# Three order sums of linear attention moved to accumulating transfers, with a reordered VectorE and ScalarE schedule

## The reference, cut to what matters

```python
h = _layernorm(x) * (1 + ca) + sa
q, k, v = split(h @ W_in.T)                      # 16 heads of 16 channels
xq, xk = clip(q / 4), clip(k / 4)
Tq, Tk = _cheb(xq), _cheb(xk)
Tv = Tk * v
kv_prefix = jnp.cumsum(Tv, axis=2)               # over the tokens, for each order
ks_prefix = jnp.cumsum(Tk.sum(axis=-1), axis=2)
num = (Tq * kv_prefix * beta).sum(axis=3)        # sum over the orders 1 to 5
den = (Tq.sum(axis=-1) * ks_prefix * beta).sum(axis=3)
x = x + ga * (num / (den + 1e-7)) @ W_out.T
h = _layernorm(x) * (1 + cb) + sb
activation = jnp.sqrt(jax.nn.softplus(h @ routing_W.T + expert_bias))
top_vals, top_idx = jax.lax.top_k(activation, 2)  # weights of the experts
x = x + gb * (shared(h) + sum over the experts of weight * expert(h))
```

## Time and profile before

| | |
|---|---|
| time, median of 3 runs | 1087.46 us (1085.91 to 1087.97) |
| profiled execution | 1086.55 us, span 1084.9 us |
| PE busy | 948.9 us (87%), 4889 matmuls |
| DVE busy | 947.9 us (87%), 1465 instructions |
| ACT busy | 472.5 us (44%) |
| POOL busy | 516.6 us (48%) |
| POOL L630, two of the sums | 32 of 2364 ns |
| DMA queues | 34.18 MB, about 13% of the time of 16 engines |

### The profile page before, as it was taken

How to read it: one execution, slowest core, us unless ns; L and a number is a source line. 1 busy time by engine, 2 the same in 40 slices (tenths; PEclk the granted TensorE clock), 3 DMA queues, 4 the chain that set the end, 5 groups by cost and what they waited for, 6 DMA issues and landing times.

```text
span 1084.9 us, 15500 instructions
## 1 busy us (share of the span) xinstructions
PE 948.9 (87%) x4889; PEld 678.4 (63%) x4889; DVE 947.9 (87%) x1465; ACT 472.5 (44%) x702; POOL 516.6 (48%) x615
## 2 busy tenths in 40 slices
PE   3864749998998989999999999898999999889996
PEld 3643436675756666675757576675757576656774
DVE  1498989999999999999999999999999999999432
ACT  4334335372635445362635444362635445441431
POOL 2032646646645546536645546536645445454210
PEclk9876869999999999999999999999999999999999
DMA  8100001020202002020202011020202010020211
GB/s 270 45 1 20 20 0 50 1 59 1 69 1 59 1 9 60 0 58 0 69 0 58 0 16 53 0 58 0 69 0 39 0 24 25 1 39 1 44 21 20
DMA packets 31517, 34.18 MB, mean 32 GB/s; under 512 B 1299, under 2 KB 30430, under 8 KB 31462
## 3 DMA queue, kind: packets, MB, share of 16 engines
q1 hardware_dynamic: 21410, 22.72, 6.3%
q0 software_dynamic: 8448, 8.39, 5.9%
q10 hardware_dynamic: 1604, 2.46, 0.7%
HBM read 16.77 MB, written 16.79 MB: 31 GB/s over the span
## 4 chain that ended last, share of the span: by engine, by line
PE 32%; DVE 30%; issue 18%; POOL 11%; ACT 3%; DVEq 1%; POOLq 0%; ACTq 0%
PE ring L1257 13%; PE acc L1394 7%; DVE feat L945 7%; PE tr L1342 4%; PE tr L1310 4%; DVE feat L966 3%; POOL feat L625 2%; DVE hid L1094 2%; DVE feat L962 2%; DVE feat L1004 2%; DVE feat L1001 2%; POOL ms L357 1%; PE tr L1248 1%; DVE route L1083 1%; PE cfb L1368 1%
## 5 line engine op out<-in xcount | busy, mean ns | idle before, releaser
L784 ACT ACTIVATE hid<-ring,b1row 128x512 f32<-128x512 f32 x144 | 98.6, 685 | 163.5 <-PE ring L1257 163.5
L630 POOL TENSOR_TENSOR feat<-feat 128x1024 f32<-128x1024 f32 x32 | 75.6, 2364 | 197.7 <-DVE feat L962 152.8
L1394 PE MATMUL acc<-w,hid 128*128 128x256 f32 x640 | 156.6, 392 | 0.0
L1394 PEld LDWEIGHTS acc<-w,hid 128*128 128x128 f32 x640 | 117.1, 191 | 28.0 <-issue 14.5
L945 DVE TENSOR_TENSOR_SCAN feat<-zero,carry,feat 128x512 f32<-128x512 f32 x80 | 113.1, 1453 | 0.0
L945 DVE TENSOR_TENSOR_SCAN feat<-zero,feat 128x512 f32<-128x512 f32 x80 | 109.9, 1413 | 0.0
L1094 DVE TENSOR_TENSOR hid<-hid,cfb 128x512 f32<-128x512 f32 x128 | 86.2, 673 | 25.7 <-PE cfb L1368 25.3
L1257 PE MATMUL ring<-n2H,w1H 128*128 128x512 f32 x288 | 101.9, 436 | 0.0
L1257 PE MATMUL ring<-n1H,winH 128*128 128x512 f32 x192 | 67.3, 433 | 38.7 <-ACT hid L784 24.9
L742 ACT ACTIVATE feat<-ring,bqkv 128x512 f32<-128x512 f32 x96 | 65.7, 686 | 71.5 <-PE ring L1257 71.5
L382 ACT ACTIVATE ntok<-xin,ms 128x256 f32 (+1 forms) x64 | 33.2, 589 | 138.5 <-POOL ms L361 138.5
(11 more groups left out here) (169 smaller groups left out, 2238.7 us busy)
## 6 DMA issues: line engine op xcount, KB each, us to landing
xin<-in_L_attn_x SPq DMA_DIRECT2D x16, 512.0 KB, 5.5
out<-x SPq DMA_DIRECT2D x16, 512.0 KB, 4.5
out<-fin POOLq DMA_DIRECT2D x16, 512.0 KB, 6.2
gates<-gate_rows SPq DMA_DIRECT2D x16, 128.0 KB, 4.8
feat<-in_L_wmod SPq DMA_DIRECT2D x1, 1536.0 KB, 14.1
feat<-in_L_attn_W_in SPq DMA_DIRECT2D x1, 768.0 KB, 9.5
const<-in_constants ACTq DMA_DIRECT2D x1, 690.5 KB, 4.3
fin<-in_constants ACTq DMA_DIRECT2D x1, 512.0 KB, 5.2
```

What stands on the lines that cost most here:

```text
L630: g.tensor_tensor(f(W + 2 * n), f(W + 2 * n), f(W + 2 * n + 1), ALU.add).then_inc(added, 1)
L784: a.activation(hid[:, e % NG], ring[bank][:, :], ACT.Silu, bias=b1row[:, e:e + 1]).then_inc(ring_copied, 1)
L1394: last = mm(acc[t // 2][:, t % 2], x[:, t * P:(t + 1) * P], w[:, e // 2], start=False, stop=(e == E), skip_group_check=True)
```

## The change

The adds of POOL go, and so does one of DVE's two. Three transfers on POOL's queue take their place: W += W+1 after two products, W+4 += W+3 after four, and, once both have landed, W += W+4. The third stands behind `exps` in POOL's list, ahead of `inv_std` of the first norm. DVE adds only W+2, after the fifth product. Orders are now scanned as 1, 2, 4, 5, 3. The copies of the last column of p = 0 are three (`carry_over`) instead of five. DVE's order changes: both scans of orders 4 and 5 stand behind `expert(3)`, their products behind `expert(4)`, then `low(4)`, `logit_parts`, the denominators, the weighing of order 3, the first norm's statistics and the clips; `finish_numerator` stands ahead of `expert(8)`. The softplus polynomial has five fitted coefficients in place of eight of the series: 10 instructions instead of 13. On ScalarE `normalise_first` moves from ahead of `silu(5)` to behind `high(6)`, and the squares of the keys from behind `silu(8)` to behind `silu(6)`.

```diff
+LOG1P = (2.0000000076817583, 0.666663216413768, 0.40024595230747134, 0.2796515774481493, 0.2815777836368378)
@@ GpSimd
             def add_orders(i, p, n):
-                pool.wait_ge(products, ND * number(i, p) + 2 * n + 2)
-                g.tensor_tensor(f(W + 2 * n), f(W + 2 * n), f(W + 2 * n + 1), ALU.add).then_inc(added, 1)
+                c = number(i, p)
+                if n < 2:
+                    pool.wait_ge(products, ND * c + 2 * n + 2)
+                else:
+                    pool.wait_ge(added[0], 16 * c + 16)
+                    pool.wait_ge(added[1], 16 * c + 16)
+                into, of = ((W, W + 1), (W + 4, W + 3), (W, W + 4))[n]
+                pool.sem_inc(sum_begun, 1)
+                g.dma_start(f(into), f(of), accum_op=ALU.add).then_inc(added[n], 16)
...
                     add_orders(i, p, 0)
+                    add_orders(i, p, 1)
+                if st["second"]:
+                    exps(*later(i, p, -1))
+                if st["attn"]:
+                    add_orders(i, p, 2)
                 if st["norm"]:
                     inv_std(pool, 0, *later(i, p, 2))
                 if st["second"]:
-                    exps(*later(i, p, -1))
                     scores(*later(i, p, -1))
-                if st["attn"]:
-                    add_orders(i, p, 1)
@@ ScalarE, in step
-                if st["norm"]:
-                    normalise_first(act, *later(i, p, 2))
                 silu(5)
                 high(4)
                 copy("v0")
                 copy("v1")
                 silu(6)
+                if qkv:
+                    for which in range(3):
+                        square(*nxt, 0, which)
                 silu(7)
                 high(6)
+                if st["norm"]:
+                    normalise_first(act, *later(i, p, 2))
                 silu(8)
                 if qkv:
-                    for q in range(2):
-                        for which in range(3):
-                            square(*nxt, q, which)
+                    for which in range(3):
+                        square(*nxt, 1, which)
@@ VectorE
-            ORDERS = (0, 1, 3, 2, 4)
+            ORDERS = (0, 1, 3, 4, 2)
+            BY_WEIGHT = (0, 1, 3, 2)
+            NCARRY, CARRIED = 3, {0: 1, 1: 1, 3: 2, 4: 2, 2: 3}
...
+            def carry_over(i, p, k):
                 if p == 0:
-                    dve.wait_ge(scanned, ND * c + j + 1)
-                    v.tensor_copy(carry[:, n], feat[:, W + n, :, CT - 1]).then_inc(carried, 1)
+                    at, n, j = ((0, 2, 1), (3, 2, 3), (2, 1, 4))[k]
+                    dve.wait_ge(scanned, ND * number(i, p) + j + 1)
+                    v.tensor_copy(carry[:, at:at + n], feat[:, W + at:W + at + n, :, CT - 1]).then_inc(carried, 1)
...
                 dve.wait_ge(products, ND * c + ND)
-                dve.wait_ge(added, 2 * c + 1)
-                v.tensor_tensor(f(W), f(W), f(W + 4), ALU.add).then_inc(numerator, 1)
-                dve.wait_ge(numerator, 2 * c + 1)
-                dve.wait_ge(added, 2 * c + 2)
+                dve.wait_ge(added[2], 16 * c + 16)
                 v.tensor_tensor(f(W), f(W), f(W + 2), ALU.add).then_inc(numerator, 1)
@@ VectorE, step, from expert(3) on (without the conditions)
                 expert(3)
+                prefix(i, p, 2)
+                prefix(i, p, 3)
+                expert(4)
+                carry_over(i, p, 1)
+                order_product(i, p, 2)
+                order_product(i, p, 3)
+                low(4)
+                logit_parts(*prev)
+                den_key_sums(i, p)
+                den_products(i, p)
+                weigh(i, p, 3)
                 token_stats(dve, 0, *after2)
-                weigh(i, p, 3)
-                prefix(i, p, 2)
                 clip(*nxt, use, 0)
                 clip(*nxt, use, 1)
-                logit_parts(*prev)
-                expert(4)
-                den_key_sums(i, p)
-                den_products(i, p)
-                low(4)
+                expert(5)
                 softplus(*prev)
-                prefix(i, p, 3)
-                expert(5)
-                order_product(i, p, 2)
-                order_product(i, p, 3)
                 invert(i, p)
                 expert(6)
+                prefix(i, p, 4)
+                low(6)
+                carry_over(i, p, 2)
+                order_product(i, p, 4)
+                expert(7)
                 combine_weights(*prev)
-                low(6)
-                prefix(i, p, 4)
-                expert(7)
-                order_product(i, p, 4)
+                finish_numerator(i, p)
                 expert(8)
-                finish_numerator(i, p)
                 divide(i, p)
```

More of the change, by code:

```diff
@@ L240, in build @@
         products = sem("order_products")
-        added = sem("orders_added")
+        added = [sem(f"orders_added{n}") for n in range(3)]
+        sum_begun = sem("order_sums_begun")
         numerator = sem("numerator")
@@ L260, in build @@
         ffn_gated = sem("ffn_gated")
-        NLOG, NSOFT, NCF, NSPLIT, NMV = 7, 13, 3, 7, 11
+        NLOG, NSOFT, NCF, NSPLIT, NMV = 7, 10, 3, 7, 11
         late_products, late_biases, late_weights = (sem(f"late_{n}") for n in ("bias_products", "biases", "weights"))
@@ L623, in weigh_order_5 @@
                 pool.wait_ge(odd_ready, 4 * c + 2)
-                ge(pool, numerator, 2 * c)
+                ge(pool, numerator, c)
                 g.tensor_tensor(f(W + 4), f(KT5), f(V0), ALU.mult).then_inc(weighted5, 1)
             def add_orders(i, p, n):
-                pool.wait_ge(products, ND * number(i, p) + 2 * n + 2)
-                g.tensor_tensor(f(W + 2 * n), f(W + 2 * n), f(W + 2 * n + 1), ALU.add).then_inc(added, 1)
+                c = number(i, p)
[7 more added lines that the diff above has]
+                g.dma_start(f(into), f(of), accum_op=ALU.add).then_inc(added[n], 16)
             def exps(i, p):
@@ L700, in step @@
                 if st["second"]:
-                    exps(*later(i, p, -1))
                     scores(*later(i, p, -1))
-                if st["attn"]:
-                    add_orders(i, p, 1)
-                if st["second"]:
                     split_weights(*later(i, p, -1))
@@ L752, in square @@
                     act.wait_ge(clipped, 2 * c + q + 1)
+                    ge(act, summed, 2 * c - 1 + q)
                     if q == 0:
-                        ge(act, summed, 2 * c)
+                        ge(act, weighted, (ND - 1) * c)
+                        ge(act, weighted5, c)
+                    else:
                         ge(act, products, ND * c)
@@ L938, in prefix @@
                 if n < 4:
-                    dve.wait_ge(weighted, (ND - 1) * c + j + 1)
+                    dve.wait_ge(weighted, (ND - 1) * c + BY_WEIGHT.index(n) + 1)
                 else:
@@ L942, in prefix @@
                 if p:
-                    dve.wait_ge(carried, ND * i + j + 1)
+                    dve.wait_ge(carried, NCARRY * i + CARRIED[n])
                 for h in range(KD):
@@ L1007, in divide @@
                 c = number(i, p)
-                dve.wait_ge(numerator, 2 * c + 2)
+                dve.wait_ge(numerator, c + 1)
                 for k in range(KD):
@@ L1062, in softplus @@
                 v.tensor_tensor(b(Z2), b(Z), b(Z), ALU.mult).then_inc(soft_steps, 1)
[L1063 to L1069, removed]
+                v.scalar_tensor_tensor(out=b(PL), in0=b(Z), scalar=LOG1P[4], in1=b(Z),
+                                       op0=ALU.mult, op1=ALU.mult).then_inc(soft_steps, 1)
+                for k, m in enumerate((3, 2, 1)):
+                    dve.wait_ge(soft_steps, at + 5 + k)
+                    v.scalar_tensor_tensor(out=b(PL), in0=b(PL), scalar=LOG1P[m], in1=b(Z2),
                                            op0=ALU.add, op1=ALU.mult).then_inc(soft_steps, 1)
-                dve.wait_ge(soft_steps, at + 11)
-                v.scalar_tensor_tensor(out=b(PL), in0=b(PL), scalar=2.0, in1=b(Z),
+                dve.wait_ge(soft_steps, at + 8)
+                v.scalar_tensor_tensor(out=b(PL), in0=b(PL), scalar=LOG1P[0], in1=b(Z),
                                        op0=ALU.add, op1=ALU.mult).then_inc(soft_steps, 1)
-                dve.wait_ge(soft_steps, at + 12)
+                dve.wait_ge(soft_steps, at + 9)
                 v.tensor_tensor(b(PL), b(PL), b(MX), ALU.add).then_inc(soft_steps, 1)
@@ L1140, in step @@
                 low(2)
+                if attn_:
+                    carry_over(i, p, 0)
                 if second:
@@ L1146, in step @@
                 expert(3)
+                if attn_:
+                    prefix(i, p, 2)
+                    prefix(i, p, 3)
+                expert(4)
+                if attn_:
+                    carry_over(i, p, 1)
+                    order_product(i, p, 2)
+                    order_product(i, p, 3)
+                low(4)
+                if second:
+                    logit_parts(*prev)
```

(15 more changed lines are left out.)

6 lines of the change are left out of this document (3 added, 3 removed).

## The result

The changed kernel takes 1103.49 us (median of 4 runs, 1101.39 to 1104.84) against 1086.68 us before on the same terms: ratio 1.0153, 95% interval 1.0131 to 1.0174. It is slower by 1.5%; the forecast was faster by 2.2%, and the time lies outside the range. Yet most of what the forecast counted did come. First its page: busy time and share of the span by engine; the new transfers' instruction on POOL (busy us, mean ns, idle before it); their KB each and median us to landing.

A forecast was written before the change was run, and what follows sets the result against it. PE and DVE were taken to bound each step together. From 1086.55 us, less 19.8 for the loop's steps and 9 for those outside, plus 5 for PE's clock, came 1062.8, called 1063, range 1055 to 1071.

The forecast's parts named there:

- The circle of PE and DVE: Step length: PE's 34.2 us from `project_out` to X plus 24.5 us back; 58.7 us for p = 1, 59.3 for p = 0.
- X: End of PE's spreading of the weights of expert 4, before which DVE's `expert(4)` can't begin; 34.2 us after `project_out`.
- DVE's second half: From X through DVE to `divide`: 24.61 us before, 23.8 after the change, next `project_out` at 24.5.
- The steps outside the full ones: Five steps outside the loop, given the mean gain of 1.8 us each, 9 us in all.
- The last expert's 0.7: PE's last expert starts only with `divide`: its 1.9 us of matmuls in place of 1.2 cost 0.7 us a step.
- cover (d): ACT keeps up: `normalise_first` by X + 20, `silu(8)` by X + 20.8, ahead of `expert(8)` at X + 21.8.
- Cover (b): PE after X catches up its 2.8 us of waits by `expert(8)`; lower clock costs 0.3 a mean step, 5 us in all.
- Cover (c): POOL's transfers land 6.2 us after issue; `scores` ends at X + 18 to 20.5, wanted at X + 19.9: cover 0 to 2 us.
- Rival 2: Slower: two successive transfers become the new wait, gain used up at a landing time of 9.7 us, 1160 us at 12; chance 0.12.
- Rival 1: POOL's chain is late: `scores` comes 1 us after DVE wants it, 1072 to 1083 us; chance 0.18.
- the 1.3 that I worked out from it: DVE's clips shut POOL out of SBUF, making the third transfer and what follows on POOL up to 1.3 us later.
- Contention: DVE operations slowed beside POOL's sums: 0.5 us at L932 and about 0.5 at L1083, 1.0 a step saved.

The follow-up runs named there:

- e4: Kernel before with the three transfers in place of POOL's two sums and DVE's first one, in its old order: 1109.67 us, ratio 1.0223.
- e2: Changed kernel, late weighing of order 3 multiplies by the key tile, so ScalarE's value copy waits for only three weighings: 1053.44 us, ratio 0.9697.
- e8: e1 with the last sum, `finish_numerator`, behind `expert(8)` again: 1036.62 us, ratio 0.9541.
- e1: Changed kernel with DVE's weighing of order 3 moved back ahead of the scans, behind `expert(3)`: 1037.58 us, ratio 0.9546.
- e5: e1 with POOL's two sums and DVE's second one in place of the three transfers, in the new order: 1096.31 us, ratio 1.0086.

## Why the prediction was wrong, by its own steps

**The circle of PE and DVE: right.** PE's 34.2 us from `project_out` to X holds in the full steps of the changed kernel and of every variant (33.7 to 34.0 to the start of the spreading), but for three steps of e4 in which `project_out` runs at the lower clock (35.5 to 35.8).

**DVE's second half, 24.5 us to the next `project_out`: right as a sum.** e2, which has all the work and all the places but not the value wait, shows 58.4 to 59.5 us a step for 58.7 and 59.3, and 1053.4 us for 1063. The steps outside the full ones gave 13.4 us for the 9 that I assigned, and the 5 us for the clock weren't needed. The way through this half is in part another than I laid out, though, and that the sum comes out is partly luck: I followed DVE to `divide` and put the last expert behind it, but PE runs without a wait from `spread_inverse` to `project_out`, and in e2 15.2 us from X to the one and 9.2 to the other make the same 24.4. The last expert's 0.7 is therefore no cost of its own, as e8 found.

**The step that failed is cover (d), ACT.** It followed the norm, `silu(8)` and the squares, and said nothing of `copy("v0")`. The moved piece was the weighing of order 3, and I costed it as 1.2 us of DVE's time. Its other property, that it is the last reader of V0, has a wait of its own in the code that I had: ScalarE's copy waits for all four weighings of the chunk before. Most of the working was at hand: with clips at X + 9.8 and 1.3 us of statistics ahead of them, the prediction had the weighing end at X + 8.5; the copy is possible at X + 3.6 (e2), so expert 6 is 5 us late, and PE, which I had ready with expert 5 at X + 9.8, isn't. The miss is 50 us (e2 against the changed kernel), 3.1 us a step; against the forecast it shows as 40, because the other terms were 10 us too careful. In the step shown it is 4.9 us idle and 1.3 at low clock, less the 2.9 us that PE waits later in e2 and here no more: 3.3.

**Cover (b), the clock.** I allowed 5 us for all, for waits of 2.8 us. For the kernel that I had in mind that was enough (e2: 0.98 from 300 to 600 us). The changed kernel has the longer wait in 13 steps, and behind every one of them expert 6 takes 2.86 us instead of 1.6, some 16 us in all; its mean granted clock is 0.929, in e1 0.97.

**Cover (c), the transfers: safe.** 6.2 us were taken, 4.6 measured, 4.5 to 5.7 over all 48; POOL needs 0.90 us for each, not 1.34. Rival 2's mechanism belongs to the old order (e4); its threshold of 9.7 us in the new one was never near, so no run tests it. Rival 1 falls with room to spare: in e2 `scores` ends at X + 16.1, and DVE wants it at X + 20.3.

By the rule of the Trainium skill (page "SBUF — State Buffer", section "Who interferes with whom") the clips would hold up the third transfer. In the step shown they don't meet: it is issued at 505.45, and the clips come at 506.79. In e1, where the clips come 1.1 us sooner, they do in every full step:

```profile
424.17 1.22 POOL L639 DMA_DIRECT2D feat<-feat  x1 [2.00 <-DMA feat<-feat]
424.56 1.36 DVE L917 TENSOR_SCALAR feat<-feat 128x1024 f32<-128x1024 f32 x2
```

The issue then takes 1.00 to 1.22 us instead of 0.92, the two clips 1.31 to 1.41 instead of 1.28. So the rule shows in these rows, but at 0.1 to 0.3 us for the issue and about 0.1 for the clips, not at the 1.3 that I worked out from it, and e1 is the faster kernel all the same. The most that a row shows is an issue of 1.55 us, once in e2; in the changed kernel the two overlap by more than 0.2 us only once (the issue at 943.17 takes 1.03).

**Contention: too small.** I counted 1.0 us a step for POOL's sums. In the old order the rows show 1.2; in the new one it would have been 1.8 + 1.9 = 3.7 (e5).

**The rivals.** All asked whether the gain would be covered by POOL's chain or by the transfers. None named a wait on a buffer, and "slower" had only the one mechanism that didn't occur.

## What to carry to other kernels

When a read is moved later, look for who overwrites what it read: the next write waits for the last reader, and the price is paid by whatever stands behind that write, here a matmul two engines away. Cost a moved instruction twice, once as time on its engine and once as the release of each buffer it touches. And where two engines alternate, put work of the one that arrives early ahead of the meeting point, not behind it: the same weighing is hidden ahead of `expert(4)`, costs 1.0 us a step behind it, and 4.1 us with the buffer's wait.

## What the runs showed of the hardware

An accumulating transfer of a 128 x 1024 f32 tile within SBUF lands 4.6 us after its issue (4.5 to 5.7 in 48), where one of the same size into DRAM lands after 6.2, and holds POOL for 0.90 us. With a pair of clips beside it the issue takes 1.00 to 1.22 us in e1's full steps, and the clips 1.31 to 1.41 for 1.28. A tile sum on POOL costs DVE between 0.5 and 1.9 us, by what DVE runs beside it. PE's granted clock fell to 0.50 to 0.69 in windows of 1 us, for some 3 us, after the idle time of 4.94 us in the step shown, and expert 6 is as long (2.86 us) behind all 13 such waits. In e4 it fell within `project_out` after 2.76, 2.21 and 2.75 us of idle time, and didn't after waits of 2.15 to 2.77 us in other steps, so the length of the idle time alone doesn't decide there. In e1, with no wait over 1.1 us between 300 and 900 us, it stayed at 1.00 from 300 to 600 us.
